# First four tiles' queries in two halves, and other places for the norms of tiles 4 to 15, in a one-core decoder layer

## The reference, cut to what matters

```
x = _layernorm(x + _L0_attn_ref(x, ...))            # convolution; r = x + z is normed inside: norm 0; outer norm: norm 1
x = _layernorm(x + _L0_xattn_ref(x, ctx, ctx, ...))  # softmax(q k^T) v, then Wo: norm 2
x = _layernorm(x + _L0_ffn_ref(x, ...))              # MLP + experts: norm 3
```

## Time and profile before

| | |
|---|---|
| median of 3 runs | 666.86 us |
| profiled execution, its own time | 669.38 us |
| its span, first to last instruction | 667.6 us |
| PE busy | 586.4 us (88%) |
| DVE busy | 491.3 us (74%) |
| ACT busy | 397.6 us (60%) |
| POOL busy | 310.8 us (47%) |
| PE's share of the chain that ended last | 69% |

### The profile page before, as it was taken

One profiled execution on the slowest core, in us unless ns is written; L12 is line 12 of the kernel. 1 busy time (PEld: TensorE's weight loads), 2 busy tenths in 40 slices (PEclk: granted clock), 3 DMA queues, 4 the chain that ended last, 5 costly groups with the idle time before them and its releaser, 6 DMA issues.

```text
span 667.6 us, 9604 instructions
## 1 busy us (share of the span) xinstructions
PE 586.4 (88%) x3132; PEld 381.5 (57%) x3132; DVE 491.3 (74%) x966; ACT 397.6 (60%) x554; POOL 310.8 (47%) x346
## 2 busy tenths in 40 slices
PE   5568797946787789999999999999999999998996
PEld 2235655735464545546785654776655588453585
DVE  7998963493468858988667797857879795778782
ACT  4776462221433549977647787673977773687760
POOL 0746664593513555333437352363633352753451
PEclk9769898986957769999999999999999999999999
DMA  8590325585520000000000000000000000000000
GB/s 241 213 386 12 104 73 144 144 206 59 204 111 0 1 1 0 1 0 1 1 0 9 16 2 8 1 1 0 17 8 9 0 1 1 16 10 8 0 13 20
DMA packets 19850, 34.13 MB, mean 51 GB/s; under 512 B 7264, under 2 KB 14177, under 8 KB 18337
## 3 DMA queue, kind: packets, MB, share of 16 engines
q1 hardware_dynamic: 15425, 29.32, 14.3%
q10 hardware_dynamic: 4376, 4.20, 2.1%
HBM read 21.81 MB, written 10.52 MB: 48 GB/s over the span
## 4 chain that ended last, share of the span: by engine, by line
PE 69%; DVE 13%; ACT 8%; issue 5%; DMA 2%; POOL 2%; SPq 0%; ACTq 0%; DVEq 0%; POOLq 0%
PE banks L813 22%; PE banks L903 8%; PE banks L908 8%; PE banks L858 5%; PE banks L880 4%; PE banks L835 3%; PE banks L729 3%; PE banks L870 3%; PE banks L703 2%; PE banks L844 2%; PE banks L693 2%; PE banks L758 2%; ACT arena L924 2%; PE banks L895 2%; DVE stats L1453 2%
## 5 line engine op out<-in xcount | busy, mean ns | idle before, releaser
L1249 POOL TENSOR_TENSOR arena<-arena 128x1024 f32<-128x1024 f32 x64 | 126.3, 1973 | 156.2 <-ACT arena L1122 155.1
L813 PE MATMUL banks<-arena 128*128 128x512 f32 x384 | 174.2, 596 | 5.9 <-issue 3.7
L813 PEld LDWEIGHTS banks<-arena 128*128 128x128 f32 x384 | 69.9, 190 | 83.3 <-issue 77.3
L1122 ACT ACTIVATE arena<-arena 128x1024 f32<-128x1024 f32 x64 | 73.5, 1149 | 7.5 <-DVE arena L1539 3.2
L1124 ACT ACTIVATE arena<-arena 128x1024 f32<-128x1024 f32 x64 | 73.5, 1149 | 2.1
L1541 DVE SCALAR_TENSOR_TENSOR arena<-arena 128x1024 f32<-128x1024 f32 x48 | 65.1, 1357 | 1.7
L1220 POOL TENSOR_SCALAR arena<-mv 128x1 f32<-128x1 f32 (+1 forms) x40 | 14.4, 361 | 103.9 <-DVE mv L1454 102.5
L1012 ACT COPY arena<-banks 128x512 f32<-128x512 f32 (+1 forms) x64 | 34.1, 533 | 46.1 <-PE banks L805 30.3
L903 PE MATMUL banks<-arena 128*128 128x256 f32 x256 | 58.4, 381 | 2.7 <-DVE arena L1563 1.3
L908 PE MATMUL banks<-arena 128*128 128x256 f32 x256 | 57.9, 379 | 0.0
L1026 ACT ACTIVATE tok<-tok,arena,rstd 128x256 f32<-128x256 f32 x48 | 27.9, 598 | 45.0 <-POOL arena L1225 44.1
(11 more groups left out here) (181 smaller groups left out, 1065.7 us busy)
## 6 DMA issues: line engine op xcount, KB each, us to landing
scr_x<-arena SPq DMA_DIRECT2D x16, 256.0 KB, 2.8
arena<-scr_x SPq DMA_DIRECT2D x2, 2048.0 KB, 11.3
scr_z<-arena ACTq DMA_DIRECT2D x14, 256.0 KB, 4.0
tok<-in_x SPq DMA_DIRECT2D x8, 256.0 KB, 5.2
arena<-scr_z SPq DMA_DIRECT2D x4, 512.0 KB
out<-tok SPq DMA_DIRECT2D x16, 128.0 KB, 1.7
arena<-scr_z SPq DMA_DIRECT2D x2, 640.0 KB
arena<-in_imat SPq DMA_DIRECT2D x1, 1152.0 KB, 5.4
```

The costliest lines, as they stand in the source:

```text
L813: ins = mm(bk[:, :], w[:, k, P * m:P * m + P], src[:, k, :], start=(k == 0), stop=(k == KC - 1))
L1122: fn(ebuf[m % 2], sxb[m % 2], ACT.Prelu, bias=negt[:, n % 2, h:h + 1], alpha=FAR).then_inc(s_ranked, 1)
L1249: tt(sxb[m % 2], sim[:, n % 2, h, 0:XR].unsqueeze(2).broadcast_to((P, XR, NKEYS)), sim[:, n % 2, FH + h, :].unsqueeze(1).broadcast_to((P, ...
```

## The change: what it does

The queries of the first super tile are done in two halves of 256 columns (tiles 0 and 1, then tiles 2 and 3), each when its own two tiles are transposed; `query` 0.j becomes `query` 0.j.0 and 0.j.1. `turn1` 0.0, the first half's queries and the scores of tile 0 get new places, and the five norm steps of each pair get a place each (`NORM_AT`) in place of a common start and common distances. `values` moves on POOL.

```diff
-         "ln": (-1.672, -1.4042, 0.3146, 1.2224, 1.9378, 2.3695, 3.0308, 3.1386),
-         "ln_steps": (-0.336, -0.234, 0.162, 0.013, 0.361), "tables": (0.0,),
+         "score_first": (-0.8, -0.7), "tables": (0.0,),
-         "x_bias": (11.0, 0.1), "values": (-1.0,),
+         "x_bias": (11.0, 0.1), "values": (-0.55,),
...
+NORM_AT = ((-2.008, -1.906, -1.51, -1.659, -1.311), (-1.182, -1.094, -0.925, -0.953, -0.909),
+           (-0.612, -0.5, -0.36, -0.3, 0.45), (-0.232, -0.2, 0.325, 0.4, 0.95), (1.0, 1.1, 1.35, 1.4, 1.6),
+           (1.5, 1.6, 1.85, 1.9, 2.1), (2.1, 2.2, 2.45, 2.5, 2.75), (2.6, 2.7, 2.95, 3.0, 3.2))
+FIRST_AT = {("turn1", 0): -1.087, ("query", 0): -1.08, ("turn1", 1): -0.78, ("query", 1): -0.77}
...
-            steps.append((PLACE["ln"][q] + PLACE["ln_steps"][k], (kind, q)))
+            steps.append((NORM_AT[q][k], (kind, q)))
...
-    queries(-1, 0)
+    for part_ in range(2):
+        steps.append((FIRST_AT[("turn1", part_)], ("turn1", 0, part_)))
+        for j in range(KC):
+            steps.append((FIRST_AT[("query", part_)] + 0.01 * j, ("query", 0, j, part_)))
     for h in range(2):
-        put(-1, "score", 0, h, j=h)
+        put(0, "score", 0, h, key="score_first", j=h)
...
-            def wide(key, w, m, src):
+            def wide(key, w, m, src, on=slice(0, W)):
...
-                    ins = mm(bk[:, :], w[:, k, P * m:P * m + P], src[:, k, :], start=(k == 0), stop=(k == KC - 1))
+                    ins = mm(bk[:, on], w[:, k, P * m:P * m + P], src[:, k, on], start=(k == 0), stop=(k == KC - 1))
...
-                    pe.wait_ge(s_tev, T_AT[("turn1", n, 1)] + 1)
-                    wide(step + ("a",), wq, step[2], x1T)
+                    if n == 0:
+                        pe.wait_ge(s_tev, T_AT[("turn1", 0, step[3])] + 1)
+                        wide(step + ("a",), wq, step[2], x1T, first_half(step[3]))
+                    else:
+                        pe.wait_ge(s_tev, T_AT[("turn1", n, 1)] + 1)
+                        wide(step + ("a",), wq, step[2], x1T)
...
-                    fn(qT[:, j, :], src, ACT.Identity, bias=pcol[:, j:j + 1]).then_inc(s_wact, 1)
+                    fn(qT[:, j, on], src[:, on], ACT.Identity, bias=pcol[:, j:j + 1]).then_inc(s_wact, 1)
```

More of the change, by code:

```diff
@@ L503, in w_bank, with first_half @@
             return bank[5 + u % 3]
+        def first_half(part_):
+            return slice(W // 2 * part_, W // 2 * part_ + W // 2)
         scr_x = t["scr_x"]
@@ L823, in _ @@
                 elif kind == "query":
-                    pe.wait_ge(s_tev, T_AT[("turn1", n, 1)] + 1)
-                    wide(step + ("a",), wq, step[2], x1T)
+                    if n == 0:
[4 more added lines that the diff above has]
+                        wide(step + ("a",), wq, step[2], x1T)
                 elif kind == "score":
                     hh, i, b = step[2], n % SUPER, n % B
-                    pe.wait_ge(s_wact, ACT_TURN[("query", n // SUPER, hh, "a")])
+                    if n < SUPER:
+                        pe.wait_ge(s_wact, ACT_TURN[("query", 0, hh, n // 2, "a")])
+                    else:
+                        pe.wait_ge(s_wact, ACT_TURN[("query", n // SUPER, hh, "a")])
                     if n == 0:
@@ L1051, in _ @@
                     if n:
-                        act.wait_ge(*W_DONE[W_AT[("query", n - 1, KC - 1, "a")]])
+                        last = ("query", n - 1, KC - 1, "a") if n > 1 else ("query", 0, KC - 1, 1, "a")
+                        act.wait_ge(*W_DONE[W_AT[last]])
                     turned_tokens(step, step[2], x1T)
@@ L1056, in _ @@
                     src = wide_ready(step + ("a",))
+                    on = slice(0, W) if n else first_half(step[3])
                     if n:
                         act.wait_ge(s_smm, 2 * SUPER * n)
-                    fn(qT[:, j, :], src, ACT.Identity, bias=pcol[:, j:j + 1]).then_inc(s_wact, 1)
+                    fn(qT[:, j, on], src[:, on], ACT.Identity, bias=pcol[:, j:j + 1]).then_inc(s_wact, 1)
                     own.done(s_wact)
```

## The result

The changed kernel takes 677.53 us, the median of 4 runs (676.81 to 678.96); the kernel before has 667.45 in 4 runs (665.59 to 668.08). The ratio is 1.0156, 95% interval 1.0136 to 1.0176: slower by 1.6%, some 10.4 us (9.1 to 11.7). The profiled execution of the changed kernel took 677.82 us with a span of 675.9, so the two profiled spans differ by 8.3.

A forecast was written before the change was run, and what follows sets the result against it. PE bounds the kernel from 282 us on, so a later project 3 delays the end. Its delay, 3.4 + 3.8 + 2.2 - 1.0 = 8.4 us at half clock, 4.2 at full, was taken as +7.4: 674.3 us, range 665 to 678.

The forecast's parts named there:

- Part A: Queries in halves and tile 0's first score: score 0.1 done 0.8 us earlier, 1.4 with PE at full clock.
- Part B: Up to the addition of project 0: DVE waits 3.0 us before residual 3; 3.4 us later, 1.7 at full clock.
- Part C: Project 0 to project 1: DVE waits 1.45 us, two residuals stand where one stood; 3.8 us more.
- Part D: Project 1 to project 2: DVE waits 3.95 us for dev0 6 on POOL; 2.2 us more, 1.6 at full clock.
- Part E: Project 2 to project 3, a chain through ACT's copies: 1.0 us less at half clock, 2.9 less at full.
- The quarter of the way to the full clock: Weighting of PE's clock up to project 3: between +8.4 us at half and +4.2 at full clock, taken as +7.4.
- wider range: Range forecast for the whole kernel's time, leaving out only extremes of the rival cases: 665 to 678 us.
- rival 3: Three of seven norm1 steps delay ACT's chain at 1.1 us each: +10.7 us, 677.6; chance 0.10.
- half-clock sum: Delay up to project 3's addition with PE at half clock: +8.4 us, against +4.2 at full clock.
- Rival 1: POOL's waits before residuals 3, 4 and 6 on DVE don't appear: -2 us, 664.9; chance 0.20.
- Rival 2: Half queries keep PE busier from 172 to 182 us and its clock up: +4.2 us, 671.1; chance 0.20.

## Why the prediction came out as it did

The forecast was 7.4 us more; 8.3 came by the two profiled spans and some 10 by the medians. The direction was right, and so was the mechanism of parts B to D; by its own steps:

- **Part A.** Score 0.1 ended 23.8 us after conv 0's copy in place of 25.5, a gain of 1.7 where I had 0.8 to 1.4. PE's score 0.1 ran at full clock (0.79), and conv 1's copy followed conv 0's sooner (161.54 behind 159.26, before 162.41 behind 159.64), which no part of the change touches.
- **Part B.** DVE's wait before residual 3 was 2.93 us (3.0 forecast); project 0 was added 2.0 us later than before, or 2.4 after conv 0's copy, between the 1.7 and 3.4 of the two clocks. The chain was the one walked at half clock, 4.70 us from PE's score 1.1 to the addition (4.71 walked); it began 1.4 us sooner than walked (195.97 for 197.35), since score 0.1 was done at 183.02 in place of 184.3.
- **Part C.** 16.49 us from project 0 to project 1 (16.2 forecast), with the wait of 1.46 (1.45). Without the waits on POOL it was 15.1, still 2.6 more than the 12.43 before, which fits the second residual.
- **Part D.** 18.01 (17.7 to 18.3 forecast), with the wait of 3.74 (3.95); dev1 5, halve and dev2 1 stand in front of dev0 6 as walked. The experiments that take these waits away give the 3.4, 1.4 and 3.7 us back.
- **Part E was the step that failed**: 1.0 to 2.9 us less were forecast, 0.2 more came. norm2 2 started 2.8 us behind project 2, as walked, but from there to the addition it was 11.88 us, where I took over the 11.05 of the chain with "one norm1 between them as now". It is one norm1 in either, but at another place: before, norm1 6 stood between the copies of probs 3.1 and 3.2, and attend 3's first sixteen rows ran beside it; now norm1 7 stands before the copy of query 1.1, and the copy of probs 3.1, for which twelve rows of attend wait, comes behind it (moved away, norm1 7 gave back 1.1 us). Those rows then ran at half clock. The copies as a whole did not become longer, 4.99 us from norm2 2 to the end of the last against 5.30 before; what lies behind them did, 6.89 us against 5.75. attend 3 on PE before, in which only four rows were left behind the last copy:

```profile
233.74 1.89 PE L858 MATMUL banks<-vbd,arena 128*128 128x34 f32 x16
...
235.97 0.64 PE L858 MATMUL banks<-vbd,arena 128*128 128x34 f32 x4 [0.35 <-ACT arena L1076]
```

- **The sum.** In the two profiles parts B to E came as 2.01, 4.06, 1.95 and 0.18 us, in all 8.20, against 8.4 walked at half clock. That these meet is in part luck: part B was walked 1.4 too long and part E 1.2 too short. The quarter of the way to the full clock, to 7.4, led away from it. The median, 677.53, lies above the forecast's own 671.5 to 677 and only inside the wider range; that it is beside rival 3's 677.6 is chance, since of the three norm1 steps of that rival one was in the chain. Why the medians show 10 and the spans 8.3 is not settled: the profiled execution of before was 1.9 us above its median, that of after 0.3, and the beginning of the schedule moves by up to 2.9 us between executions.
- **The clock.** The rule of the Trainium skill (TensorE: Matmul & The Clock Gate, Part 1: The HAM clock gate), that half clock is the default and activity releases it, spoke for the half-clock sum. The sum did come out nearer to 8.4 than to 4.2, and the clock stayed between its levels, at 0.60 to 0.63 from 186 to 232 us. In two of the three stretches less work of PE went with a lower clock: 0.61 and 0.60 with 11.30 and 11.27 us of work, where the kernel before had 0.66 and 0.72 with 12.65 and 11.81. But from 186 to 199 it was at 0.63 with PE working 6.30 us, against 0.50 with 12.48 before, so there less work did not mean a lower clock, and the trace bears the rule out only in part. The second stretch before:

```profile
199.00:214.00 15.00, 12.65 (x60) 8.67 (x59) 12.88 (x32) 5.79 (x11) 5.45 (x11) 0.66 0.01 1
```

- **The rivals.** Rival 1 (POOL's waits don't appear) fell: all three are in the trace with POOL as the releaser. Rival 2's clock came in places: score 0.1 and attend 0 took 0.79 and 2.32 us on PE, before 1.40 and 4.32, but DVE set the time there, and project 0 was still at 2.08. Rival 3 (three norm1 steps in ACT's chain) held for one, norm1 7, at 1.1.

## What to carry to other kernels

An engine that works off its list in order passes a wait on: before a step is moved, look at what stands in front of its supplier's step on the other engine's list and what that waits for; a swap of two POOL steps gave back 3.4 us at project 0. Where other engines' steps leave room for one piece of work on an engine and not for two, spread it, one piece to a round, and let the rest follow where the engine waits anyway: tile 1 took 12.4 us with one residual, 15.1 with two and no wait on POOL, and 11.1 with one right behind the projection. The places in one list are compared after each engine's own lag has been added, so the order that counts is the sorted one, not that of the numbers in the table.

## What the runs showed that I had not expected

The same twelve rows of attend 3 in the same order took 1.53 us in three kernels and 2.47 to 2.77 in two, with the granted clock of tile 3's stretch at 0.81 to 1.00 and at 0.73 to 0.76. Just before, PE had waited 1.03 to 1.34 us for the first score of tile 4 in the three and 1.60 in the two. What set the level was not tried. From project 2 to project 3 the two took 14.4 and 14.7 us and the three 11.9 to 13.5, so 0.9 to 2.8 us went with it, and the later rise behind project 3 above went with another 1.9: as much as single waits under study.
